# Moving the folding of the value and output weights from the first stage of a decoder kernel into its latents' stage

## The reference

```python
x = x + attn(layernorm(x), q_proj_w, kv_a_proj_w, kv_a_ln_w, kv_b_proj_w, o_proj_w)

compressed = hidden_states @ kv_a_proj_w.T                  # 128 latent values and 64 rotary ones
kv = rmsnorm(compressed[..., :128], kv_a_ln_w) @ kv_b_proj_w.T
k_pass, v = kv[..., :128], kv[..., 128:]                    # per head, 16 heads
out = softmax(q @ k * scaling, causal) @ v
return out @ o_proj_w.T
```

## Time and profile before

| what | value |
|---|---|
| median of 3 runs | 2401.43 us |
| lowest, highest | 2400.1, 2414.57 us |
| the profiled execution | 2410.91 us |
| its span | 2409.2 us |
| mean granted TensorE clock | 0.945 of full speed |
| stage 1 and stage 2 in its trace | 0 to 55.97 us, 55.97 to 125.4 us |

### The profile page before, as it was taken

The page is one execution under the profiler, slowest core; times in us unless marked ns, Lnnn a source line. Parts: engine busy times, 40 slices in busy tenths (PEclk is TensorE's granted clock), DMA queues, the critical chain, the costliest instruction groups (busy, mean ns, idle before and its releaser), DMA issues. The chain is left out here.

```text
span 2409.2 us, 37756 instructions
## 1 busy us (share of the span) xinstructions
PE 2118.4 (88%) x11216; PEld 1771.7 (74%) x11216; DVE 1495.5 (62%) x3096; ACT 1008.4 (42%) x2038; POOL 946.8 (39%) x948
## 2 busy tenths in 40 slices
PE   5689999995799999589999999999998799659991
PEld 3578888883577777478888888888887678547771
DVE  3635555555888888357767777777776456535554
ACT  2323333333332332245666655656656322136660
POOL 1400000000666666435344343434342455346664
PEclk9899999997899999799999999999999899769995
DMA  8621212116254454332222222222211344163336
GB/s 294 167 82 35 66 35 65 39 35 214 84 153 140 141 157 156 97 119 64 65 68 76 76 64 67 60 67 63 81 51 35 115 105 119 37 231 119 108 101 201
DMA packets 293925, 244.04 MB, mean 101 GB/s; under 512 B 151906, under 2 KB 258898, under 8 KB 290386
## 3 DMA queue, kind: packets, MB, share of 16 engines
q1 hardware_dynamic: 273186, 190.42, 27.1%
q10 hardware_dynamic: 14160, 34.22, 3.9%
q0 software_dynamic: 6496, 18.37, 2.8%
HBM read 149.42 MB, written 93.53 MB: 101 GB/s over the span
## 5 line engine op out<-in xcount | busy, mean ns | idle before, releaser
L2207 ACT ACTIVATE ca_prob<-ca_ps_s,ca_down,ca_scales 112x487 f32<-112x487 f32 x256 | 194.1, 758 | 241.3 <-DVE ca_down L2334 241.3
L2016 POOL TENSOR_TENSOR ca_k<-ca_k 125x512 f32<-125x512 f32 x64 | 82.9, 1296 | 347.3 <-DVE ca_k L2297 347.3
L2330 DVE TENSOR_REDUCE ca_top<-ca_ps_s 112x1 f32<-112x487 f32 x256 | 168.3, 657 | 41.4 <-PE ca_ps_s L77 41.4
L75 PE MATMUL ca_ps_p<-ca_w_hi,ca_c_hi 128*125 128x512 f32 x384 | 159.5, 415 | 28.0 <-POOL ca_c_lo L2005 28.0
L599 POOL COPY sa_val<-lat_v 112x128 f32<-112x128 f32 (+1 forms) x64 | 18.9, 296 | 410.5 <-PE sa_ps_o L656 410.2
L76 PE MATMUL out_ps_y<-out_w_lo,out_o_hi 128*128 128x512 f32 x448 | 179.1, 400 | 0.0
L75 PE MATMUL out_ps_y<-out_w_hi,out_o_hi 128*128 128x512 f32 x308 | 129.6, 421 | 40.4 <-DVE out_o_lo L1208 15.9
L77 PE MATMUL ca_ps_p<-ca_w_hi,ca_c_lo 128*125 128x512 f32 x384 | 155.0, 404 | 0.0
L76 PE MATMUL ca_ps_p<-ca_w_lo,ca_c_hi 128*125 128x512 f32 x384 | 154.8, 403 | 0.0
L2324 DVE TENSOR_TENSOR ca_pT_lo<-ca_ps_t,ca_pT_hi 125x448 fp32r<-125x448 f32 x256 | 152.7, 616 | 2.3 <-ACT ca_pT_hi L2215 2.3
L2106 PEld LDWEIGHTS ca_ps_t<-ca_ident,ca_prob 112*125 112x125 f32 x1024 | 131.8, 188 | 19.1 <-ACT ca_prob L2207 11.3
(11 more groups left out here) (314 smaller groups left out, 6553.4 us busy)
## 6 DMA issues: line engine op xcount, KB each, us to landing
self_outT<-sa_ov SPq DMA_DIRECT2D x64, 224.0 KB, 2.4
out_o_raw<-self_outT SPq DMA_DIRECT2D x56, 256.0 KB, 2.9
cross_qT<-out_qt SPq DMA_DIRECT2D x56, 256.0 KB, 2.6
ca_q_raw<-cross_qT SPq DMA_DIRECT2D x64, 224.0 KB, 2.8
cross_outT<-ca_ov SPq DMA_DIRECT2D x64, 224.0 KB, 3.0
out_o_raw<-cross_outT SPq DMA_DIRECT2D x56, 256.0 KB, 4.1
ffn_raw<-in_expert_w SPq DMA_DIRECT2D x8, 1536.0 KB
ca_c_first<-in_ctxT SPq DMA_DIRECT2D x15, 750.0 KB
```

Of the source, the lines that this page charges most:

```text
L75: pe.matmul(out, a_hi, b_hi, start=start, stop=False)
L2016: pool.tensor_tensor(k1[0:m, :], k1[0:m, :], k2[0:m, :], ALU.add).then_inc(k_added.sem, 1)
L2207: act.activation(prob[j % 2][:, 0:KV], ps_s[j % 2][:, 0:KV], ACT.Exp, bias=down[:, j:j + 1], scale=scales[par][:, n:n + 1], accum_out=tota ...
L2330: dve.tensor_reduce(top[:, j:j + 1], ps_s[j % 2][:, 0:KV], AX.X, ALU.max, negate=True).then_inc(topped.sem, 1)
```

## The change

The value-output products leave stage 1. A new class `ValueFold` holds their buffers and semaphores. In stage 1 ACT now only issues the loads: the value weights and the output weights of the first 8 heads, after the 13th group. The load of the query weights' piece moves from after the 9th group to after the 5th. In stage 2, every step i with 0 <= i < 16 does head i: PE makes the product between the latent products of batch i+1 and the transposes of batch i, ACT (not DVE) copies it after its copy into `lat_kT`, and SP stores two heads at a time. SP also loads the output weights of heads 8 to 11 and 12 to 15, at its batches 4 and 8, after waiting for the product of head 3 and head 7. Stage 2 has no hardware loop any more: all steps are written out on every engine. Its end waits for the last store of products.

```diff
@@ fold_weights, scalar
-                if n == 0:
-                    act.dma_start(vb[:, :, :], wvb).then_inc(vb_in, 16)
-                if n in (KD, 2 * KD):
-                    half = n // KD - 1
-                    act.dma_start(wo[:, half], woT[:, half * HQ:(half + 1) * HQ, :]).then_inc(wo_in[half], 16)
-                if n == 2 * KD:
+                if n == KD:
                     act.dma_start(rot[:, :, :], wq_rotT).then_inc(rot_in, 16)
+                if n == 3 * KD:
+                    values.load_first(act)
             act.wait_ge(kva_in, 16)
             act.activation(kva_hi[:, :, :], kva[:, :, :], ACT.Copy).then_inc(plain_hi, 1)
-            for c in range(2, NQ):
-                act.wait_ge(v_mm, HQ * (c - 1))
-                act.dma_start(wo[:, c % 2], woT[:, c * HQ:(c + 1) * HQ, :]).then_inc(wo_in[c % 2], 16)
-                if c == 2:
-                    act.wait_ge(rot_in, 16)
-                    act.activation(qr_hi[:, :, :], rot[:, :, :], ACT.Copy).then_inc(plain_hi, 1)
+            act.wait_ge(rot_in, 16)
+            act.activation(qr_hi[:, :, :], rot[:, :, :], ACT.Copy).then_inc(plain_hi, 1)
...
+class ValueFold(ExitStack):
+    AHEAD = 8
...
+    def load_late(self, sp, c):
+        sp.wait_ge(self.done, c * HQ + HQ - self.AHEAD)
+        self.load(sp, c)
+
+    def store(self, sp, n):
+        sp.wait_ge(self.out, n + 1)
+        at = n % HQ
+        sp.dma_start(self.vo[:, n - 1:n + 1, :], self.vos[:, at - 1:at + 1, :]).then_inc(self.stored[n // 2 % 2], 16)
+
+    def product(self, pe, n):
+        if n == 0:
+            pe.wait_ge(self.vb_in, 16)
+        if n % HQ == 0:
+            pe.wait_ge(self.wo_in[n // HQ], 16)
+        if n >= 2:
+            pe.wait_ge(self.out, n - 1)
+        pe.matmul(self.ps[n % 2][:, :], self.vb[:, n, :], self.wo[:, n % self.AHEAD, :], start=True, stop=True)\
+            .then_inc(self.done, 1)
+
+    def copy(self, eng, n):
+        eng.wait_ge(self.done, n + 1)
+        if n >= HQ and n % 2 == 0:
+            eng.wait_ge(self.stored[n // 2 % 2], 16 * (n // HQ))
+        eng.activation(self.vos[:, n % HQ, :], self.ps[n % 2][:, :], ACT.Copy).then_inc(self.out, 1)
@@ latents
-            for i in range(-3, 0):
-                step(0, i)
-            with eng.Fori(0, (B - 3) // 2) as h:
-                step(h, 0)
-                step(h, 1)
-            for i in range((B - 3) // 2 * 2, B):
+            for i in range(-3, B):
                 step(0, i)
@@ latents, sync
-            with sp.Fori(0, B // 2 - 1) as h:
-                for par in range(2):
-                    body(h * 2 + 2 + par, par)
-                    store(h * 2 + par, h, par)
-            for par in range(2):
-                store(B - 2 + par, B // 2 - 1, par)
+            for b in range(B):
+                if b + 2 < B:
+                    body(b + 2, b % 2)
+                if b in (4, 8):
+                    values.load_late(sp, b // HQ + 1)
+                store(b, b // 2, b % 2)
+                if b % 2 and b > 1:
+                    values.store(sp, b - 2)
+            values.store(sp, H - 1)
             for par in range(2):
+                sp.wait_ge(values.stored[par], 16 * H // HQ)
                 sp.wait_ge(put[par].sem, put[par].at(B // 2 - 1, 1))
@@ latents, scalar
                     act.activation(lat_kT[:, :, bass.ds(b * S, S)], ps_t[i % 2][:, :, :], ACT.Copy).then_inc(kept.sem, 1)
+                    values.copy(act, i)
@@ latents, tensor
                 if has(h, i):
+                    values.product(pe, i)
                     par = i % 2
```

More of the change, by code:

```diff
@@ L134, in identity, with fold_weights @@
                        pattern=[[-1, tile.shape[1]]], channel_multiplier=1).then_inc(sem, 1)
-def fold_weights(nc, wq_nope, wkb, wvb, woT, wq_rotT, wkvaT, qf_hi, qf_lo, qr_hi, qr_lo, kva_hi, kva_lo, scratch, vo):
+def fold_weights(nc, wq_nope, wkb, wq_rotT, wkvaT, qf_hi, qf_lo, qr_hi, qr_lo, kva_hi, kva_lo, scratch, values):
     ctx = Phase(nc, "fold")
@@ L146, in fold_weights @@
         kb = sb("kb_nat", [P, H, RANK])
-        vb = sb("vb_nat", [P, H, RANK])
-        wo = sb("wo_nat", [P, 2, HQ, D])
         rot = scratch[:, 0:KD * H * ROPE].rearrange("p (k n) -> p k n", k=KD)
         kva = sb("kva_raw", [P, KD, RANK + ROPE])
-        vos = sb("vos", [P, 2, HQ, D])
         psq = [ctx.bank(f"psq{i}", P, 512) for i in range(4)]
-        psv = [ctx.bank(f"psv{i}", P, 512) for i in range(4)]
         kb_in = [sem(f"kb_loaded{c}") for c in range(NQ)]
         wq_in = [sem("wq_loaded0"), sem("wq_loaded1")]
[L156 to L160, removed]
+        kva_in, rot_in = sem("kva_loaded"), sem("rot_loaded")
+        q_mm, q_hi, q_lo, plain_hi, plain_lo = (sem(n) for n in (
+            "q_products", "q_hi", "q_lo", "plain_hi", "plain_lo"))
         block = ctx.enter_context(nc.Block())
@@ L171, in _ @@
                 sp.dma_start(wq[:, c % 2], nope[0:NOPE, c * HQ:(c + 1) * HQ, :]).then_inc(wq_in[c % 2], 16)
[L172 to L176, removed]
         @block.gpsimd
@@ L197, in _ @@
                     mm.then_inc(q_mm, 1)
[L198 to L205, removed]
         @block.scalar
@@ L237, in _, with __init__, load, load_first @@
                                   qf_hi[:, k, c * HQ:(c + 1) * HQ, :], ALU.subtract).then_inc(q_lo, 1)
[L238 to L243, removed]
-    return ctx
+    return ctx
+class ValueFold(ExitStack):
+    AHEAD = 8
+    def __init__(self, nc, ctx, wvb, woT, vo):
+        super().__init__()
+        self.src, self.vo = (wvb, woT), vo
+        sb = lambda name, shape: ctx.enter_context(nc.sbuf_tensor(name, shape, F32))
+        self.vb = sb("vb_nat", [P, H, RANK])
+        self.wo = sb("wo_nat", [P, self.AHEAD, D])
+        self.vb_in = nc.alloc_semaphore(name="vb_loaded")
+        self.wo_in = [nc.alloc_semaphore(name=f"wo_loaded{c}") for c in range(NQ)]
+        self.sems = [self.vb_in] + self.wo_in
+    def load(self, eng, c):
+        at = c * HQ % self.AHEAD
+        eng.dma_start(self.wo[:, at:at + HQ, :], self.src[1][:, c * HQ:(c + 1) * HQ, :]).then_inc(self.wo_in[c], 16)
+    def load_first(self, eng):
+        eng.dma_start(self.vb[:, :, :], self.src[0]).then_inc(self.vb_in, 16)
+        for c in range(self.AHEAD // HQ):
+            self.load(eng, c)
+    def work(self, phase):
+        self.vos = phase.sb("vos", [P, HQ, D])
+        self.ps = [phase.bank(f"psv{i}", P, D) for i in range(2)]
+        self.done, self.out = phase.sem("v_products"), phase.sem("v_copied")
+        self.stored = [phase.sem(f"vo_stored{i}") for i in range(2)]
+    def load_late(self, sp, c):
[19 more added lines that the diff above has]
+        eng.activation(self.vos[:, n % HQ, :], self.ps[n % 2][:, :], ACT.Copy).then_inc(self.out, 1)
@@ L283, in exponent, with latents @@
     pool.wait_ge(sem, 1)
-def latents(nc, x, lnw, kva_hi, kva_lo, lat_kT, lat_v, xT_hi, xT_lo):
+def latents(nc, x, lnw, kva_hi, kva_lo, lat_kT, lat_v, xT_hi, xT_lo, values):
     W = RANK + ROPE
@@ L330, in latents @@
         kept = ev("lat_kept", 1, 2)
+        values.work(ctx)
         block = ctx.enter_context(nc.Block())
@@ L2801, in build @@
             kva = esb("kva_hi", [P, KD, RANK + ROPE], F32R), esb("kva_lo", [P, KD, RANK + ROPE], F32R)
-            fold = fold_weights(nc, q_proj, kv_heads[0], kv_heads[1], woT, wq_rotT, wkvaT, *qf, *qr, *kva,
-                                lat_kT[:, :, :].rearrange("p c t -> p (c t)"), vo)
-            lat = latents(nc, x, kv_ln, *kva, lat_kT, lat_v, *x0T)
+            values = ValueFold(nc, early, kv_heads[1], woT, vo)
+            fold = fold_weights(nc, q_proj, kv_heads[0], wq_rotT, wkvaT, *qf, *qr, *kva,
+                                lat_kT[:, :, :].rearrange("p c t -> p (c t)"), values)
+            lat = latents(nc, x, kv_ln, *kva, lat_kT, lat_v, *x0T, values)
         sa = self_attention(nc, *x0T, *qf, *qr, lat_kT, lat_v, o1T, out_w)
-    clear(nc, fold, lat, sa)
+    clear(nc, fold, values, lat, sa)
     out1 = self_output(nc, o1T, out_w, x_rows, x1, x1T, qT, q_scales,
```

## The result

The changed kernel took 2418.27 us (median of 6 runs, 2416.84 to 2424.74) against 2407.44 us for the kernel before (6 runs, 2400.1 to 2414.57): a ratio of 1.0051 with a 95% interval of 1.0027 to 1.0076. It is slower by half a percent, within the 1% that the chances called no change, but above the forecast of 2404 and just above the range. (The six runs of before also put its median 6 us above the three shown first.) Measured again later, beside two experiments, the ratio was 1.0025, 1.0014 to 1.0036.

The account below looks back on a forecast made before the run. Stage 1 was taken as bound by transfers, stage 2 by a chain of dependent steps; -10.3 - 1.3 + 7.4 + 2 + 4.8 = +2.6 us on the 2401.4 us median gave 2404 us, range 2389 to 2418.

Parts of the forecast that it names:

- the chances: Whole kernel against a 1% (24 us) threshold: faster 0.03, same 0.93, slower 0.04.
- stage 1: Stage 1 without products, copies and stores: the next stage begins at 45.7 instead of 55.97, -10.3 us (-12.3 to -8.3).
- late loads: Stage 2, SP's batches 4 and 8: waiting for a head's product delays x by 3.7 us each, +7.4 us (4.8 to 9.2).
- loop and the store before x: Stage 2: written-out steps gain, stores ahead of every second x load cost; 3.77 us per batch, -1.3 us with the entry.
- clock: Stage 2: each stall may bring one more spell of PE at half clock, about two batches, +2 us (0 to 6).
- end: End of stage 2: last copy, its 512 KB store and landing precede the next stage's loads, +4.8 us (3.6 to 7.0).
- the upper end: Stage 2, one late load: x waits for the 1 MB issued before it and lands at 90.0, 4.6 us late.
- the sign of 12 us at half clock: Clock windows of stage 2: more than 12 us at 0.50 would speak for PE becoming the bound.
- The second rival: Stage 2: PE at half clock becomes the bound in most of 13 middle batches, +15 us, 2417 us; chance 0.10.
- The first: Rival, stage 2: the late loads wait for nothing, -6.8 us, 2395 us, or 2392 with full unrolling; chance 0.22.
- The third: Rival, stage 2: loads of x late at every second batch, +5 in place of -1.3, +9 us, 2410 us; chance 0.08.
- Later stages: Stages after stage 2: same data in the same order, costed at nothing.

Follow-up runs that it names:

- second execution of the change: The changed kernel itself run once more, beside the two combinations: 2417.53 us, ratio 1.0025 to the kernel before.
- The reordered kernels: The change with the 2 MB piece and the three product loads issued later in stage 1: alone 2409.8 us, within two combinations 2398.78 and 2399.63 us.
- the run without the wait: The change with its two 1 MB late loads moved to SP's batches 6 and 10, their products long made: 2413.41 us, ratio 1.0012 to before.

## Why the prediction was wrong

Its mechanism held: stage 1 shorter, twice a stall at the late loads, a wait at the end. The sizes failed, of stage 1 and the late loads above all, both in the same direction. Of the 14.3 us between 2404 and 2418.27, 6.0 are the median of three runs that stood for the kernel before (2401.43, and 2407.44 with six); the rest is the change, +10.8 us in the medians where the sum was +2.6. Term by term, from the two traces:

| term | predicted | measured | how |
|---|---|---|---|
| stage 1 | -10.3 | -6.0 | 49.95 - 55.97 |
| late loads | +7.4 | +10.9 | intervals of the scales of batches 7 and 11 (8.68, 9.51) less 3.64 each |
| loop and the store before x | -1.3 | 0.0 | -2.8 for 12 intervals and the entry, +2.8 at batches 6, 10, 14 |
| clock | +2 | +1.2 | excess at batches 8, 9, 12, 13 |
| end | +4.8 | +3.8 | 4.65 less the 0.85 before |
| start and tail of stage 2 | none | +0.6 | 5.42 against 5.67 us to the first scale, 7.10 against 6.26 from the last |
| sum | +2.6 | +10.5 | first load 10.45 us later |

In the second execution of the change the sum is +8.2: the late loads +10.1, the store before x +2.1 instead of 2.8, the clock +0.3; the rest is the same within 0.1.

- **Stage 1, the step that failed most.** The prediction saw that the 2 MB piece goes ahead of the fourth chunk, but let it cost 2 us at worst and nothing in the sum. The chunk landed 11.6 us after its issue instead of 8.6, and PE waited 5.93 us (4.13 in the second execution, with the stage's end at the same 49.95). With the piece behind it the chunk landed after 5.5 us, and that alone gave 3.8 us. The issuing of three loads was put at 1.5 us; it took 3.4, and 3.05 us of the stage were its share in the experiments. The reordered kernels begin stage 2 at 43.1 and below, so even -10.3 was less than the move allows. That the DMA engines are full there was read in the earlier trace rows, and then not applied to what the change issues.
- **The late loads.** Position and cause were right, and x was a victim; that ACT would wait as long for the store of batch 4 was not seen. The price of one was 5.45 us, not 3.7, above even the 4.6 taken as the upper end. The wait and the megabyte add, as the run without the wait shows. x of batch 7 landed 6.0 us after its issue, against a median of 2.9 before, and 2.0 us after the megabyte (issued at 76.14, landed 5.7 us later); the upper end had let both land together. That the data stores stood in the same line was named, and not priced. The Trainium skill ("DMA: Bandwidth & Descriptors", "Queues, rings and completion order") says that each DMA engine consumes the descriptors of one ring in order. The trace agrees, and the 4.6 us that the prediction drew from this rule were nearer to 5.45 than its middle.
- **The loop and the store before x.** The prediction computed an average of 3.77 us per batch. The batches ran at 3.64 instead, and the store cost 0.7 to 1.1 us at each of three batches, which took back the 2.8 us that writing out the loop gave.
- **The clock.** Right in kind: half clock after each stall, PE full for one to two batches. It cost 1.2 us in all, 0.3 in the second execution, not 2. Its working misread: 5.18 us of 6.40 make 3.1 us of a batch of 3.875, not 3.3; and the 11.3 us of half clock are two windows only, beside which the 20.40 us at 0.92 hold another 3.3 us. So the sign of 12 us at half clock tells nothing. The second rival, a clock that stays low, is excluded: with the product and without late loads (all weights in stage 1) the granted clock is 1.00 from 65 to 115 us.
- **The rivals.** The first (late loads that wait for nothing) is out by the gaps; the slower one gave the right total, 2417, by a mechanism that did not occur, which is luck. The third (x late at every second batch) holds for batches 6, 10 and 14 only, 2.8 us together.
- **Later stages** cost nothing that shows: 1.5 us less in one execution, which is inside their scatter.

## What to carry to other kernels

Work moved into another stage's idle engines can be free there and still lose, through the transfers that it brings: each new transfer must be priced by what stands behind it in its queue and by what it stands ahead of on the DMA engines. A wait put on an issuing engine delays everything that engine would have issued, so load in small pieces, at points where the wait is long satisfied. An issue itself can hold up the engine that makes it, and what it costs is not told by the DMA share: before, ACT issued 1 MB in 0.33 us at 24.05, with the DMA share at 1.08 in that moment; in the change the issue of two such loads, behind a load that ACT had just issued, took 2.46 us, though the DMA share was 0.00 when the first of the three began. Put several large loads that follow each other in one queue behind that engine's last work in the stage.

## What the hardware showed that was not expected

The issue of a 1 MB load took ACT 0.33 to 0.35 us in the kernel before, but 2.46 us for two of them in the change and 4.79 us for two with the 2 MB piece of the same queue still under way; on SP the issue of a 512 KB store took 0.35 to 0.65 us in other places, and 1.71 and 1.84 us behind the late loads and what SP had queued after them. What in the queue sets this cost is open: in the kernel before, the 2 MB piece issued straight behind 1 MB took 0.54 us. Writing out a loop of two batches took 0.235 us off each batch (3.875 to 3.64), in a chain of five engines, without any fetch stall visible.
